# Edge pairs spread by TensorE, x loaded in parts, w0's products pipelined, and another order for the last tiles of a graph transformer's front

## The chip, the cores and the metric

The kernel runs on 1 core of a Trainium2 chip. The metric is device time in microseconds (us); smaller is better. Three runs of the kernel before took 3420.39, 3433.01 and 3434.41 us, median 3433.01.

## The reference

The inputs are x (2500 nodes x 512), and 40000 edges (src, dst), sorted by dst. What is computed:

```
deg  = max(number of edges into each node, 1);  norm = deg ** -0.5
h    = relu(layernorm(x))
x    = x + relu(norm * segment_sum((norm * (h @ w0))[src], dst) + bias0)
h    = relu(layernorm(x))
two layers, 8 heads of 64:
   q, k, v = h @ Wq.T + bq, h @ Wk.T, h @ Wv.T
   p = softmax over the edges of each target node of q[tgt].k[src] / 8
   h = batchnorm(h + segment_sum(p * v[src]) @ Wo.T + bo);  h = batchnorm(h + feed_forward(h))
out  = x + layernorm(h)
```

## The kernel before, in words

Nothing is gathered by edge. A matrix of counts (2500 x 2500, how often an edge src to dst occurs) is built in HBM, and it serves both parts: the first convolution is counts times hw, and the attention is dense, over all 2500 nodes, with log(count) added to the scores and a very low value where the count is zero.

The program has a front (function `front`, lines 191 to 907) and a transformer, which are blocks with a barrier between them. Nodes are handled in NT = 20 tiles of P = 125. The front has these stages.

1. **The matrix of counts.** DVE writes a tile of zeros (L533) and ScalarE's queue sends it to the table in HBM 8 times (L695, 25.0 MB in all). GpSimd then adds the edges to the table by 320 indirect DMAs of 125 edges each (L500), 160 groups of 2 on 2 sides of the table; the next group of a side waits until that side's last has landed, and the first waits until all zeros have. Each DMA needs cells and counts that `tallies(k)` on DVE makes (L509 to L531): 40 blocks of 8 columns. A column compares its 125 pairs (dst*2500+src) with the 250 pairs of its group (L518), which lie in `pair_row`, the same row in all 125 partitions. That row comes by DMA: the pairs are stored to HBM (`pair_flat`) and each block's 1000 pairs are loaded back by a DMA that repeats them over the partitions, two blocks in flight.
2. **Degrees and due times.** One-hot rows of dst (L555) are multiplied on TensorE (L809) for the degrees; `below` and `needed` (L565 to L588) work out which group is the last that a tile of nodes needs. As edges are sorted, tile t needs about 8(t+1) groups, 16(t+1) of the 320 indirect DMAs. The degrees go through HBM into column form (L704, L706), and norm follows (L598).
3. **h @ w0.** x is loaded whole by ScalarE's queue (L697), after the 8 issues of zeros and without a wait. Statistics of x (L577, L580), then a loop over tiles: ScalarE makes h (L716), TensorE turns it (L825), ScalarE copies it (L721), TensorE multiplies by w0 (L831), ScalarE scales the product into `hw` (L723), and only then begins the next tile. DVE meanwhile works off the tallies of blocks AHEAD = 5 to 39.
4. **The tile loop.** When all hw are there (`first_done`), SP loads w_q, w_k, w_v and three tiles of x, and then, for each tile t, the two halves of its count rows (`parts`, L114, "keys<-counts" in the trace), once GpSimd has landed the group that the tile needs. Two tiles are in flight. DVE merges the halves (L656), makes the bias of the attention (L665, L671), TensorE turns the counts (L843, 5 chunks) and multiplies them with hw (L853, 5 times 4 products of two passes), DVE finishes the convolution (L611 to L626), ScalarE normalises (L746). The projections of tile t-1 (L860, L871 twice, L879) stand between the chunks of tile t on TensorE. Results go to HBM: q, k, v in two f16 halves, the bias rows, x1.
5. **The end.** SP waits until tiles 0 to 17 are stored, fetches keys of heads 0 to 3 (L400) after the last merge, then keys of heads 4 to 7, and all values after the last product; tiles 18 and 19 go straight from SBUF to keys and values. `keys` and `values` lend their room to the front until then (w0, parts and cnt in keys, hw in values). At the end of the block SP waits for all bias, q and x1 stores and for the straight copies.

The attention begins with SP's load of q (L1208) and of 10 pieces of the bias (L1214). TensorE's first score waits for all keys, its first weighing for all values.

The order of each engine is written out by hand, and a later instruction of a queue is never run ahead of an earlier one that waits. On SP:

```
for t in range(NT + 3):
    store_bias(t - 2) ... store_q(t - 3), store_k(t - 3) ... store_x1(t - 2), store_v(t - 3)
    load_x(t + 1)
    sp.wait_ge(groups_landed, last_group)      # of tile t
    load_rows(sp, parts[t % 2] ...)
```

Of the kernel before, what the change touches and what calls it, by code (L numbers as in the profile page):

```python
# [17 lines left out]
F32 = mybir.dt.float32  # L18
F16 = mybir.dt.float16
BF16 = mybir.dt.bfloat16  # L20
# [9 lines left out]
D = 512  # L30
# [22 lines left out]

EARLY = 2
AHEAD = 5
# [81 lines left out]
def gnn_kernel(nc, x, src_cols, dst_cols, src_runs, dst_runs, w0, bias0, wq, wk, wv, wo, w1, w2,  # L137
# [17 lines left out]
    pair_flat = dram("pair_flat", [1, E], F32)  # L155
# [7 lines left out]
    with top:  # L163
# [10 lines left out]
        keys_early, keys_late = sem("keys_early"), sem("keys_late")  # L174
        values_early, values_late = sem("values_early"), sem("values_late")
# [4 lines left out]
def front(nc, sem, psum, sb, g):  # L180
    x, w0, bias0, xt = g["x"], g["w0"], g["bias0"], g["xt"]
    src_cols, dst_cols, src_runs, dst_runs = g["src_cols"], g["dst_cols"], g["src_runs"], g["dst_runs"]
    counts, bias_rows, x1_rows = g["counts"], g["bias_rows"], g["x1_rows"]
    pair_flat, deg_flat = g["pair_flat"], g["deg_flat"]
# [3 lines left out]
    keys_early, keys_late, values_early, values_late = g["keys_early"], g["keys_late"], g["values_early"], g["values_late"]  # L188
    XR = 4

    STRAIGHT = 2
    STAGED = NT - STRAIGHT
# [4 lines left out]
    HALVES = 2  # L197
    TH = NT // HALVES
# [5 lines left out]
    with ExitStack() as ctx:  # L204

        hw = values[:, :, :, :].rearrange("p h t e -> p (h t e)").bitcast(F32).rearrange("p (t d) -> p t d", t=NT)
        parts = [keys[0:P, 2 * b:2 * b + 2, :].rearrange("p h n -> p (h n)").bitcast(U16) for b in range(2)]
        cnt = [keys[0:P, 4 + 2 * b:6 + 2 * b, :].rearrange("p h n -> p (h n)").bitcast(F32) for b in range(2)]
# [14 lines left out]
        with ExitStack() as first:  # L223
            x_sb = sb(first, "x_sb", [P, NT, D])

            room = keys[:, :, :].rearrange("p h n -> p (h n)")
            w0_sb = room[:, 0:2 * FC * D].bitcast(F32).rearrange("p (c d) -> p c d", c=FC)
            room = room[0:EP, 2 * FC * D:].bitcast(BF16)
            onehot_hi = [room[:, b * QC * HI:(b + 1) * QC * HI].rearrange("p (c w) -> p c w", w=HI) for b in range(2)]
            room = room[:, 2 * QC * HI:]  # L230
            onehot_lo = [room[:, b * QC * LO:(b + 1) * QC * LO].rearrange("p (c w) -> p c w", w=LO) for b in range(2)]
            below = room[:, 2 * QC * LO:2 * QC * LO + TH * NCOL].rearrange("p (t c) -> p t c", t=TH)
# [5 lines left out]
            ramp_i = sb(first, "ramp_i", [EP, LO], I32)  # L238
            ramp = sb(first, "ramp", [EP, LO], BF16)
# [6 lines left out]
            src_run_i = sb(first, "src_run_i", [EP, NCOL], I32)  # L246
            dst_run_i = sb(first, "dst_run_i", [EP, NCOL], I32)
# [27 lines left out]
        with ExitStack() as first:  # L275
            deg_ps = psum(first, "deg_ps", [HI, LO])
            needed_ps = psum(first, "needed_ps", [NT, 2 * 128])
# [1533 lines left out]
```

## Time and profile before

| what | us |
|---|---|
| median of 3 runs | 3433.01 |
| the profiled execution | 3420.37 |
| its span in the profile | 3418.6 |
| TensorE busy | 3044.7 (89%) |
| GpSimd busy | 2156.7 (63%) |
| first indirect DMA begins | 72.96 |
| first h of the w0 loop | 130.64 |
| first merge of counts | 291.29 |
| last indirect DMA begins | 908.0 |
| attention's first product | 992.63 |

The page gives one execution. Busy time of an engine is summed over the whole span, so a stage must be read in windows. In a line of the timeline the numbers are the start, the length, the engine (a q behind it means its queue, which issues), the line, what is written and read, the count, and in brackets the idle time before it with what ended it.

### The profile page before, as it was taken

To read this page: it belongs to the slowest core of one execution; us is meant where nothing else is said; L and a number is where in the kernel's file an instruction comes from. 1 tells how busy PE (TensorE), PEld (TensorE's weight loads), DVE (VectorE), ACT (ScalarE), POOL (GpSimd) and SP (SyncE) were. 2 spreads that over 40 slices of the span, in tenths; PEclk is the share of its full clock that TensorE was granted. 3 is DMA by queue.
4 is the path that set the end of the run, shared out by engine and by line. 5 is a ranking of instruction groups with operands and counts; after the bars stand their busy time and mean duration, and the time that the engine had idled before them with its cause. 6 is when DMAs were issued, how large, how long until landed. Compare 5 with 4: busy or idle time off the path is not lost. (4 is left out here: it accounts for less than half of the span.)

```text
span 3418.6 us, 72329 instructions
## 1 busy us (share of the span) xinstructions
PE 3044.7 (89%) x24802; PEld 2394.4 (70%) x24802; DVE 2269.7 (66%) x6951; ACT 1953.9 (57%) x3918; POOL 2156.7 (63%) x1979
## 2 busy tenths in 40 slices
PE   2367999998769999999999989989999999999985
PEld 2123656654448888888888877767888888888874
DVE  8694344432237888888888853237888888888856
ACT  0123444443337778777777721227778778777734
POOL 1687888887527777777777710017777777777734
PEclk9998999998889999999999999999999999999998
DMA  9656666654479999999999821239999999889951
GB/s 372 99 129 139 122 133 117 125 104 90 111 181 175 165 170 169 166 166 175 165 163 165 152 74 31 54 72 175 168 165 168 168 171 170 166 163 168 158 122 60
DMA packets 1297433, 496.25 MB, mean 145 GB/s; under 512 B 1237211, under 2 KB 1262836, under 8 KB 1291379
## 3 DMA queue, kind: packets, MB, share of 16 engines
q1 hardware_dynamic: 1156168, 459.71, 67.3%
q0 software_dynamic: 133120, 0.80, 4.0%
q10 hardware_dynamic: 7788, 31.21, 2.8%
q8 instruction: 196, 3.21, 0.4%
q14 instruction: 161, 1.32, 0.1%
HBM read 153.04 MB, written 79.96 MB: 68 GB/s over the span
## 5 line engine op out<-in xcount | busy, mean ns | idle before, releaser
L1422 DVE CUSTOM_DVE_ANT_0 prob<-s_ps,mask 125x500 f32<-125x500 f32 x1600 | 1057.9, 673 | 286.0 <-PE s_ps L1267 207.9
L1199 POOL TENSOR_TENSOR staged<-prob,staged 125x500 f16<-125x500 f32 x960 | 1065.8, 1116 | 156.8 <-ACT staged L1193 94.7
L1359 ACT ACTIVATE prob<-prob,neg_max 125x1000 f32<-125x1000 f32 (+1 forms) x960 | 954.6, 994 | 114.5 <-DVE scrap L1428 112.8
L1267 PE MATMUL s_ps<-keys,queries 128*125 128x500 f16 x3200 | 945.7, 378 | 41.4 <-DMA queries<-q_tiles 29.2
L500 POOL DMA_INDIRECT counts<-count,cell x320 | 657.5, 2055 | 245.7 <-issue 107.5
L1300 PEld LDWEIGHTS o_ps<-values,across 125*125 125x125 f16 x7680 | 591.3, 138 | 200.5 <-issue 58.2
L1300 PE MATMUL o_ps<-values,across 125*125 125x128 f16 x7680 | 607.0, 222 | 38.2 <-DMA across<-staged 37.6
L1193 POOL CAST staged<-prob 125x500 f16<-125x500 f32 x640 | 385.6, 602 | 376.0 <-ACT prob L1359 252.8
L1435 DVE TENSOR_TENSOR p_lo<-t_ps,p_hi 125x500 f16<-125x500 f32 x640 | 432.0, 675 | 91.1 <-ACT p_hi L1369 90.8
L1278 PE MATMUL t_ps<-identity,prob 125*125 125x125 f32 x2560 | 412.5, 284 | 2.5 <-ACT agg L1379 2.2
L1369 ACT CAST p_hi<-t_ps 125x500 f16<-125x500 f32 x640 | 361.2, 564 | 85.9 <-PE t_ps L1278 85.6
L1267 PEld LDWEIGHTS s_ps<-keys,queries 128*125 128x125 f16 x3200 | 354.8, 139 | 54.5 <-DMA queries<-q_tiles 30.8
L853 PE MATMUL agg_ps<-values,turned 125*125 125x512 f32 x800 | 369.4, 605 | 4.3 <-ACT turned L730 3.4
L1300 PE MATMUL o_ps<-values,p_hi 125*125 125x128 f16 x2560 | 364.5, 221 | 1.5 <-DVE p_lo L1435 1.5
L1300 PE MATMUL o_ps<-values,p_lo 125*125 125x128 f16 x2560 | 363.4, 221 | 0.0
L1300 PEld LDWEIGHTS o_ps<-values,p_hi 125*125 125x125 f16 x2560 | 321.9, 137 | 51.6 <-DVE p_lo L1435 2.5
L1300 PEld LDWEIGHTS o_ps<-values,p_lo 125*125 125x125 f16 x2560 | 310.9, 138 | 47.0 <-issue 0.2
L1193 ACT CAST staged<-prob 125x500 f16<-125x500 f32 x320 | 195.7, 611 | 246.8 <-issue 188.5
L1278 PEld LDWEIGHTS t_ps<-identity,prob 125*125 125x125 f32 x2560 | 331.5, 189 | 6.0 <-ACT prob L1359 3.3
L853 PEld LDWEIGHTS agg_ps<-values,turned 125*125 125x125 f32 x800 | 145.6, 192 | 158.1 <-issue 157.6
L1248 POOL MEMSET staged<- 128x1024 f16 x6 | 5.5, 951 | 386.4 <-POOLq L999 308.6
L1359 ACT ACTIVATION_READ_ACCUMULATOR prob<-prob,neg_max 125x1 f32 x960 | 185.5, 193 | 0.0
(152 smaller groups left out, 3499.3 us busy)
## 6 DMA issues: line engine op xcount, KB each, us to landing
mask<-bias_rows SPq DMA_DIRECT2D x200, 218.8 KB
counts<-xt ACTq DMA_DIRECT2D x8, 3054.0 KB, 37.2
keys<-counts SPq DMA_DIRECT2D x40, 546.9 KB
bias_rows<-edge_bias SPq DMA_DIRECT2D x20, 1093.8 KB
queries<-q_tiles SPq DMA_DIRECT2D x80, 250.0 KB, 3.8
pair_row<-pair_flat SPq DMA_DIRECT2D x40, 437.5 KB
across<-staged SPq DMA_TRANSPOSE x960, 3.3
q_tiles<-q_both SPq DMA_DIRECT2D x80, 125.0 KB, 2.7
```

Source lines behind the costliest of these rows:

```text
L500: pool.indirect_dma_start(counts, bass.IndirectOffsetOnAxis(cell[:, c:c + 1], 0), count[:, c:c + 1], None, compute_op=ALU.add).then_inc(gr ...
L853: mm = pe.matmul(agg_ps[t % 2][0:P, :], lhsT=turned_sb[u % 2][0:P, j * P:(j + 1) * P], rhs=hw[:, s, :], start=(s == 0), stop=(s == NT - 1))
L1193: copy(staged[n % STAGES][0:P, 0:BPC, 0:P], prob[u % PROBS][:, k * KC:(k + 1) * KC].rearrange("p (s c) -> p s c", s=BPC)).then_inc(high_st ...
L1199: engine.tensor_tensor(here[0:P, BPC:2 * BPC, 0:P], prob[u % PROBS][:, k * KC:(k + 1) * KC].rearrange("p (s c) -> p s c", s=BPC), here[0:P ...
L1248: pool.memset(staged[r][:, :, :], 0).then_inc(stages_cleared, 1)
L1267: mm = pe.matmul(s_ps[n % SB][:, 0:KC], lhsT=queries[b][:, h, part, :], rhs=keys[:, h, c * KC:(c + 1) * KC], start=(part == 0), stop=(part ...
L1278: mm = pe.transpose(t_ps[r][0:P, s * P:(s + 1) * P], prob[u % PROBS][:, (k * BPC + s) * P:(k * BPC + s + 1) * P], identity[0:P, 0:P])
L1300: mm = pe.matmul(o_ps[u % 2][:, 0:2 * DH], lhsT=weights[:, s * step:s * step + P], rhs=values[:, u % H, k * BPC + s, :], start=(k == 0 and ...
L1359: act.activation(here, here, ACT.Exp, bias=neg_max[u % 4][:, :], accum_out=sums[u // H % 2][:, u % H, piece:piece + 1]).then_inc(exped, 1)
L1369: act.copy(p_hi[m % PB][:, :], t_ps[r][0:P, 0:KC]).then_inc(p_high, 1)
L1422: dve.tensor_tensor_reduce(out=prob[u % PROBS][:, at], in0=s_ps[n % SB][:, 0:KC], in1=bias[b][:, at], scale=1.0, scalar=MASKED, op0=ALU.ad ...
L1435: dve.tensor_tensor(p_lo[m % PB][:, :], t_ps[r][0:P, 0:KC], p_hi[m % PB][:, :], ALU.subtract).then_inc(bank_read, 1)
```

## The change

All of it is in `front`, but for two waits in the attention.

- Pairs' rows: the two extra loads of the edges, the store to `pair_flat` and 80 loads of `pair_row` (40 blocks in two cuts) are gone. TensorE makes a row of 500 pairs by 4 transposes of a column repeated 125 times, into two banks of PSUM, from which DVE's comparisons read. 80 such rows stand in TensorE's order, 30 ahead of the w0 loop and 50 inside it.
- x comes in four parts, issued after all zeros have landed, two in flight. DVE does the statistics of a part, then the tallies of a block. AHEAD goes from 5 to 10; 14 blocks are tallied ahead of h. The degrees' trip through HBM is issued by SP, early.
- The due times come from a smallest dst for each column, by transposes; the one-hot rows have their columns innermost.
- The w0 loop is skewed: ScalarE and TensorE turn tile t+1 before they multiply tile t. hw lies in the upper halves of keys and values, parts and cnt in the lower ones.
- SP loads the parts of tile 0 ahead of the weights and x, the parts of tile 1 behind them.
- From tile APART = 17 on, the projections of tile t-1 stand wholly ahead of the sums of tile t, on all engines.
- Only tile 19 goes straight to keys and values. Heads 0 and 1 are fetched when tiles 0 to 18 are stored, heads 2 and 3 after the last merge and the last bias, heads 4 to 7 after the last product. The first score waits for heads 0 to 3, the fifth unit's for the others.

The core of the diff:

```diff
-AHEAD = 5
+AHEAD = 10
+XPARTS = 4
+LAST_AHEAD = AHEAD + XPARTS - 1
-    STRAIGHT = 2
-    STAGED = NT - STRAIGHT
+    STAGED = NT - 1
+    APART = 17
 SP:
-                sp.wait_ge(pairs_ready, 1)
-                store_rows(sp, pair_flat.rearrange("o (p c) -> (o p) c", p=EP), pair_run[:, :], pairs_stored)
-                for k in range(NB):
-                    if k >= 2:
-                        sp.wait_ge(rows_used, k - 1)
-                    load_rows(sp, pair_row[k % 2][:, :], pair_flat[:, at].broadcast_to([EP, PER_ROW * GE]), rows_loaded[k % 2])
+                load_parts(0)
                 load_weights(sp, weights, 0, weights_loaded)
                 for t in range(XR - 1):
                     load_x(t)
+                load_parts(1)
+                for t in range(2, APART):
+                    store_bias(t - 2)
+                    if t >= 3:
+                        store_q(t - 3)
+                        store_k(t - 3)
+                    store_x1(t - 2)
+                    if t >= 3:
+                        store_v(t - 3)
+                    load_x(t + 1)
+                    load_parts(t)
+                store_q(APART - 3)
+                store_k(APART - 3)
+                store_v(APART - 3)
+                for t in range(APART, NT):
+                    if t == APART:
+                        store_bias(t - 2)
+                        store_x1(t - 2)
+                    if t + 1 < NT:
+                        load_x(t + 1)
+                    store_q(t - 2)
+                    store_k(t - 2)
+                    store_v(t - 2)
+                    store_bias(t - 1)
+                    store_x1(t - 1)
+                    load_parts(t)
+                store_q(NT - 2)
+                store_k(NT - 2)
+                store_v(NT - 2)
+                for b in range(2):
+                    sp.wait_ge(qkv_stored[b], QKV * len(range(b, STAGED, 2)))
+                keys_back(range(2), first_heads)
+                values_back(0, 2, first_heads)
+                sp.wait_ge(merged, NKC * NT)
+                keys_back(range(2, 4), first_heads)
+                store_bias(NT - 1)
+                values_back(2, 4, first_heads)
+                sp.wait_ge(cnt_t_used, NKC * NT)
+                keys_back(range(4, H), last_heads)
+                values_back(4, H, last_heads)
+                store_x1(NT - 1)
+                store_q(NT - 1)
+                keys_straight(NT - 1)
+                values_straight(NT - 1)
 DVE:
+                def tally_column(at):
+                    if at % RC == 0:
+                        dve.wait_ge(rows_turned, row + 1)
+                    dve.scalar_tensor_tensor(
+                        matches[at % 2][:, :], row_ps[row % 2][0:EP, own * GE:(own + 1) * GE], pair[:, at:at + 1],
+                        earlier[:, after:after + GE], ALU.is_equal, ALU.mult, accum_out=tally[:, at:at + 1]).then_inc(tallied, 1)
+                for part in range(XPARTS):
+                    x_statistics(part)
+                    if part + 1 < XPARTS:
+                        tallies(AHEAD + part)
+                for t in range(APART - 1, NT):
+                    if t >= APART:
+                        merge(t)
                         least(t)
                         mask(t)
                         convolve(t)
+                    low_q(t)
+                    low_k(t)
+                    low_v(t)
 ScalarE:
+                act.wait_ge(zeroed, 16 * ZDMAS)
+                for part in range(XPARTS):
+                    if part >= 2:
+                        act.wait_ge(x_loaded[part % 2], BOTH * (part // 2))
+                    load_rows(act, x_sb[:, tiles, :], x.rearrange("(t p) d -> p t d", p=P)[:, tiles, :], x_loaded[part % 2])
+                first_norm(0)
+                first_norm(1)
+                keep_ht(0)
+                for t in range(NT):
+                    if t + 1 < NT:
+                        keep_ht(t + 1)
+                    if t + 2 < NT:
+                        first_norm(t + 2)
+                    keep_hw(t)
 TensorE:
+                def spread_row(n):
+                    if n >= 2:
+                        pe.wait_ge(tallied, RC * (n - 1))
+                    for c in range(RC):
+                        mm = pe.transpose(row_ps[n % 2][0:EP, c * EP:(c + 1) * EP],
+                                          pair[:, n * RC + c:n * RC + c + 1].broadcast_to([EP, EP]), identity[0:EP, 0:EP])
+                    mm.then_inc(rows_turned, 1)
+                for t in range(NT):
+                    if t + 1 < NT:
+                        turn_h(t + 1)
+                    times_w0(t)
+                    for n in range(done + (NROW - done) * t // NT, done + (NROW - done) * (t + 1) // NT):
+                        spread_row(n)
+                def project_all(t):
+                    turn_x1(t)
+                    pe.wait_ge(xt_ready, t + 1)
+                    project(t, "wq_sb", q_ps, q_summed, q_scaled, FC)
+                    project(t, "wk_sb", k_ps, k_summed, k_low, 1)
+                    project_v(t)
+                for t in range(NT):
+                    between = 1 <= t < APART
+                    if t >= APART:
+                        project_all(t - 1)
 ...
+                project_all(NT - 1)
 attention, TensorE:
-                        pe.wait_ge(g["keys_early"], H * 16)
+                        pe.wait_ge(g["first_heads"], 4 * 16 + 2 * BOTH)
+                    if layer == 0 and u == H // 2 and c == 0:
+                        pe.wait_ge(g["last_heads"], 4 * 16 + BOTH)
-                    if layer == 0 and u == 0 and k == 0:
-                        pe.wait_ge(g["values_early"], 2 * BOTH)
```

## Rows read from the trace of the kernel before

**Rows 1.** SP's issues in the timeline, loads of parts of tiles 15 to 19

```profile
743.49 1.58 SPq L114 DMA_DIRECT2D keys<-counts  x4
...
869.43 1.58 SPq L114 DMA_DIRECT2D keys<-counts  x4
...
911.79 1.59 SPq L114 DMA_DIRECT2D keys<-counts  x4
```

**Rows 2.** L500 alone, 742 to 911 us: durations, starts, idle time before

```profile
L500 POOL DMA_INDIRECT counts<-count,cell x64: 1982/1986/2477, 742.1 to 908.0; - x64
...
  DMA counts<-count,cell: 15.0, 4
```

**Rows 3.** L500 alone, 318.6 to 742 us

```profile
L500 POOL DMA_INDIRECT counts<-count,cell x167: 1982/2000/2488, 318.6 to 739.8; - x167
```

**Rows 4.** Timeline of TensorE in the tile loop: turning of x1, tiles 1 and 11

```profile
353.36 0.59 PE L860 MATMUL x_ps<-identity,h 125*128 125x125 f32 x4
...
662.51 0.59 PE L860 MATMUL x_ps<-identity,h 125*128 125x125 f32 x4
```

**Rows 5.** Timeline of the start of the program and of the tile loop

```profile
72.96 2.13 POOL L500 DMA_INDIRECT counts<-count,cell  x1 [66.22 <-DMA counts<-xt]
...
107.91 11.96 DVE L577 BATCH_NORM_STATS2 stats<-x_sb 125x6 f32<-125x512 f32 x20 [22.23 <-DMA x_sb<-x]
...
130.64 0.81 ACT L716 ACTIVATE h<-x_sb,shift,rstd 125x512 f32<-125x512 f32 x1 [0.41 <-DVE norm L598]
...
291.29 3.04 DVE L656 TENSOR_TENSOR keys<-keys 125x500 f32<-125x500 uint16 x5 [21.85 <-DMA keys<-counts]
```

**Rows 6.** Windows: length, PE and PEld, DVE, ACT, POOL busy, clock, DMA share, GB/s

```profile
4.00:73.00 69.00, 18.95 (x321) 17.43 (x321) 66.26 (x108) 0.00 (x0) 2.78 (x5) 1.00 1.01 410
73.00:108.00 35.00, 0.00 (x0) 0.00 (x0) 6.96 (x37) 0.00 (x0) 12.52 (x7) 1.00 1.09 192
...
946.00:988.00 42.00, 20.64 (x92) 13.75 (x91) 6.12 (x12) 7.26 (x14) 0.22 (x1) 0.77 0.96 237
```

**Rows 7.** L500 alone, 80 to 110 us, and 0 to 277.5 us

```profile
  DMA counts<-count,cell: 21.3, 2
...
L500 POOL DMA_INDIRECT counts<-count,cell x77: 1982/2058/2212, 73.0 to 274.1; - x77
```

**Rows 8.** Timeline of GpSimd around first_done

```profile
284.28 1.99 POOL L500 DMA_INDIRECT counts<-count,cell  x1 [8.24 <-DMA counts<-count,cell]
...
297.51 2.00 POOL L500 DMA_INDIRECT counts<-count,cell  x1 [6.67 <-issue]
```

**Rows 9.** Timeline of TensorE, tile 18's sums

```profile
877.98 2.04 PE L843 MATMUL turn_ps<-identity,keys 125*125 125x125 f32 x8 [10.12 <-DVE keys L656]
879.94 5.45 PE L853 MATMUL agg_ps<-values,turned 125*125 125x512 f32 x8
...
907.85 3.60 PE L879 MATMUL v_ps<-wv_sb,xt 128*125 128x512 f32 x8
```

**Rows 10.** The same of tile 19's last steps, and the attention's first product

```profile
956.39 1.09 PE L860 MATMUL x_ps<-identity,h 125*128 125x125 f32 x4 [3.52 <-ACT h L746]
958.15 5.67 PE L871 MATMUL q_ps<-xt,wq_sb 128*128 128x125 f32 x32 [0.67 <-ACT xt L753]
...
967.24 3.60 PE L879 MATMUL v_ps<-wv_sb,xt 128*125 128x512 f32 x8
992.63 2.76 PE L1267 MATMUL s_ps<-keys,queries 128*125 128x500 f16 x6 [21.80 <-DMA queries<-q_tiles]
```

**Rows 11.** Timeline of DVE: tile 19's convolution, the last half of v

```profile
949.47 0.75 DVE L611 SCALAR_TENSOR_TENSOR conv<-agg_ps,norm,bias_sb 125x512 f32<-125x512 f32 x1 [2.15 <-PE agg_ps L853]
...
951.89 0.18 DVE L622 BATCH_NORM_AGGREGATE x_mv<-x_stats 125x2 f32<-125x6 f32 x1
...
971.49 0.69 DVE L643 TENSOR_TENSOR v_both<-v_ps,v_both 125x512 f16<-125x512 f32 x1 [2.77 <-ACT v_both L775]
```

**Rows 12.** Timeline of ScalarE: tile 19's root, before its h

```profile
954.80 0.29 ACT L744 ACTIVATE x_root<-x_mv,eps_col 125x1 f32<-125x1 f32 x1
```

More of the change, by code:

```diff
@@ L245, in front @@
             group_i = sb(first, "group_i", [EP, NCOL], I32)
-            src_run_i = sb(first, "src_run_i", [EP, NCOL], I32)
-            dst_run_i = sb(first, "dst_run_i", [EP, NCOL], I32)
-            pair_run = sb(first, "pair_run", [EP, NCOL])
-            pair_row = [sb(first, f"pair_row{b}", [EP, PER_ROW * GE]) for b in range(2)]
             matches = [sb(first, f"matches{r}", [EP, GE], BF16) for r in range(2)]
@@ L527, in tallies, with place_block @@
                                                         ALU.is_lt, ALU.mult))
-                    steps.wait(but=1)
-                    steps.done(dve.tensor_tensor(cell[:, at], moved[:, :], home[:, at], ALU.add))
+                def place_block(k):
+                    at = slice(k * BC, (k + 1) * BC)
                     steps.wait()
-                    dve.sem_inc(cells_ready, 1)
+                    dve.tensor_tensor(cell[:, at], moved[:, :], home[:, at], ALU.add).then_inc(cells_ready, 1)
@@ new lines, in tallies, with x_statistics @@
+                def tallies(k):
+                    for c in range(BC):
+                        tally_column(k * BC + c)
+                        if c == 2 and k >= 1:
+                            count_block(k - 1)
+                        if c == 4 and k >= 1:
+                            place_block(k - 1)
+                def x_statistics(part):
+                    dve.wait_ge(x_loaded[part % 2], BOTH * (part // 2 + 1))
+                    for t in range(part * XT, (part + 1) * XT):
+                        steps.done(dve.bn_stats(stats[:, t, :], x_sb[:, t, :]))
@@ L791, in _ @@
+                high_v(APART - 2)
+                for t in range(APART - 1, NT):
+                    if t >= APART:
+                        for k in range(3):
+                            chunk(t, k)
                         logarithm(t)
[L792 to L794 removed]
                         chunk(t, 3)
[L796 to L798 removed]
@@ L806, in _ @@
+                pe.wait_ge(consts_ready, 3)
+                pe.wait_ge(pairs_ready, 2)
+                spread_row(0)
+                spread_row(1)
+                for c in range(3):
+                    columns = slice(128 * c, min(128 * (c + 1), NCOL))
+                    mm = pe.transpose(dst_ps[0:columns.stop - columns.start, c * EP:(c + 1) * EP], dst[:, columns], identity[0:EP, 0:EP])
+                mm.then_inc(needed_turned, 1)
                 for q in range(QP):
```

381 lines of the change are left out of this document (187 added, 194 removed).

## The prediction

> **What bounds the kernel now.** I began with the loads of count rows on SP. The spacing of tiles 15 to 19 is (911.79 - 743.49) / 4 = 42.1 us [rows 1]. Further forward the spacing of two turnings of x1, ten tiles apart, is (662.51 - 353.36) / 10 = 30.9 us [rows 4], so there TensorE had work without a gap, and later it did not: tile 18's sums start after 10.1 us of idleness [rows 9]. Next I looked at GpSimd alone. An indirect DMA takes 1.99 us and 0.30 us to the next, 2.29 us as the floor; 167 of them take 423.5 us in the first stretch (2.54 each) and 64 take 167.9 us in the second (2.62 each), the last begins at 908.0 [rows 2, 3], and tile 19 is loaded 3.8 us later [rows 1]. A tile needs 16 of them, 16 x 2.62 = 42 us. So from about tile 12 on the scatter of edges sets the pace, and the end of the front is the end of the scatter and a tail: from tile 19's load at 911.8 to the attention's first product at 992.6, 80.8 us [rows 1, 10]. The scatter has one start, at 72.96, when the last zeros have landed [rows 5]. The reader should see in these rows that the chain of the front is zeros, 320 indirect DMAs, tail, and that x, tallies and the w0 loop lie beside it.
>
> How much slack lies there? TensorE could run the 19 tiles behind the first in 19 x 30.9 = 587 us, so from 291.3 [rows 5] the last would start at 878, and its counts come at 920 (911.8 and 8.1 to land and merge, by tile 18: 869.43 to 877.98 is 8.5) [rows 1, 9]. Some 40 us of the stage before the tile loop are covered already.
>
> **The change part by part.** The sum is made against the profiled execution, 3420.4 us with a span of 3418.6; the median of the three runs is 12.6 above it, and I add that at the end. About 0.5%, 17 us, is what a measurement of this kernel can tell from no change.
>
> *w0 loop, due times, one-hot rows, x in parts, seen from TensorE.* Now the loop runs from 130.6 to about 272. A tile's 8 products take 3.6 us at the full clock and up to 5.45 at the lower one [rows 9], say 4.2; 50 rows of 4 transposes stand in the new loop, at the 0.15 us of one of x1's four [rows 4] 30 us in all; with turning 0.6 us, 4.2 + 0.6 + 1.5 = 6.3 us a tile, 126 us, against 20 x 7.1. DVE's comparisons go on there, 26 blocks instead of 35, which now fit into the loop's 141 us, so at most 105 us, beside it; that they read PSUM now may lengthen them by a fifth before they bound the loop. The start moves from 130.6 to about 105: the statistics end at 119.9 [rows 5], of which x's landing gives some 10 us and their overlap with it another 9; what lies between them and h, 10.7 us, shrinks by the degrees' trip, which is made earlier. That puts first_done near 230, and with the parts of tile 0 ahead of 3 MB of weights the first merge near 240 instead of 291. All of these 50 us I cost at nothing: the cover is the scatter; if it were gone, the loop would end the front in both kernels and the 50 us would come through. Tile t of the loop starts at 240 + 30.9 t, its counts come at about 920 - 42 (19 - t); the two cross at tile 11, so eight or nine tiles go at the scatter's pace instead of four or five.
>
> *Zeros.* Until 73 the DMA engines are full (share 1.01, 410 GB/s) [rows 6]. 25.0 MB of zeros take 61 us of that; about 5 blocks of pair_row (2.4 MB) and the edges' loads go with them. Without pair_row, 2.4 / 0.41 = 6 us less: the scatter starts at 66.5. -6.5.
>
> *x beside the scatter's start.* From 73 to 108 the engines moved 6.7 MB [rows 6], x and w0 and about a megabyte of pair_row, and two indirect DMAs waited 21.3 us together [rows 7]. x is no longer queued before the scatter, but it is issued at the very time at which the scatter starts, so the same bytes less one in seven lie beside it. Bounds: nothing waits (-20.7), or no DMA lands for all 35 us (+8, as four would have gone in the 21.3 case beyond the waits). I take 21 x 6/7 = 17, -3.7, as nearest to the row.
>
> *Tallies beside the scatter.* From 73.0 to 274.1 there are 76 intervals, 174 us at the floor; of the 27 us more the two waits are 20.7, so 6.4 go to the time in which DVE tallies [rows 7]. Tallies end a fifth of that time earlier. -1.4.
>
> *The burst at first_done* (weights, x, parts) costs the scatter 8.24 + 6.67 less two gaps, 14.3 us [rows 8]. It stays. 0.
>
> *Tiles beside the scatter.* Over the floor, the first stretch lost 423.5 - 382.4 = 41 us to 13.7 tiles, 3.0 each, the second 167.9 - 146.6 = 21 us to 4 tiles, 5.3 each [rows 2, 3]: there the parts' load and all the stores of a tile come in one burst right behind a landing. With 8 instead of 4 tiles in that regime, +9.1.
>
> So tile 19's load moves by -6.5 - 3.7 - 1.4 + 9.1 = -2.5 us, to 909.3.
>
> *The last tiles' order.* Tile 16 is still interleaved. From its sums' start to the last add is 29.9 us and to the end of project_v 33.4 (877.98 to 907.85, where project_v starts, to 911.4) [rows 9]. From 17 on each tile is a serial ring: sums 20.1 us (first product at 1.5, 5 of 3.46, three turnings of 0.43; 22.4 where it begins cold as in [rows 9]), I take 21.2; then convolution, norm and h on DVE and ScalarE, 4.2 us (2.6 from 949.47 to the variance's end at 952.07, 1.6 from the root at 954.80 to the turning) [rows 11, 12]; then turning and three projections, 956.39 to 970.84, 14.4 us [rows 10]; then v's halves and the merge that DVE now makes behind them, 2.1 us (970.84 to 972.18, and 0.7) [rows 10, 11]. Sum 41.9 us, against the scatter's 42. Tile 17's sums start 8.5 + 29.9 + 4.2 + 14.4 + 2.1 + 2.8 (project_v of 15 before normalise) = 61.9 us after load 16, that is 19.9 after load 17, 11.4 later than its counts. As ring and pace are equal this lag stays: tile 19's sums end 19.9 + 21.2 = 41.1 us behind its load, where they now end at 949.4, 37.6 behind. +3.5. What was bought is that no other work lies in tile 19's sums, and it is paid for by the lag of tiles 17 and 18.
> The rows show the cost of such pauses: after 10.1 us of idleness the first 8 products take 5.45 us and later ones 3.60 [rows 9]; after 3.5 us of idleness q takes 5.67 [rows 10]. The Trainium skill (TensorE: Matmul & The Clock Gate, Why this matters for your kernels) says to leave no idle gaps between bursts of products, since the clock then falls from 2.4 to 1.2 GHz. The ring has two pauses a tile, 4.2 and 2.1 us; by the rule the cold values would hold for both, 22.4 + 4.2 + 14.4 + 2.1 = 43.1 us a ring, and the sums would end 3 us later still. This case's trace agrees for the pause of 3.5 us, and the mean granted clock there is 0.77 [rows 6].
>
> *After the last product.* Now 9.9 MB move between 946 and 988 (237 GB/s, share 0.96) [rows 6]: bias, half of the keys, all values, two tiles' q, k, v. The first product waits 21.8 us after the last projection [rows 10]. So DMA bounds this. In the new order keys and values of heads 0 and 1 and keys of 2 and 3 go earlier; behind the last product remain bias 1.25 MB, values of 2 and 3 1.2, heads 4 to 7 4.8, and 1.0 of q, k, v, x1: 8.25 MB, 32.6 us instead of 38.8 at the same rate. The block's end waits for the straight copies, which SP issues behind them on its queue, so that the later wait on heads 4 to 7 gives nothing of its own. 43.2 us from sums to first product become 37. -6.1.
>
> Sum: -2.5 + 3.5 - 6.1 = -5.1 us. The attention behind it is the same. 3420.4 - 5 = 3415, and on the median 3433 - 5 = 3428.
>
> **The rivals.**
> *A. The scatter goes at its better rate, and the lag is gone.* If tiles go on costing it 3.0 us and not 5.3 (8 x 2.3 = 18 us), or if the pace is slow enough to swallow the lag (sums at 8.5 + 21.2 = 29.7 us behind the load, -11.4), or if x in parts frees the scatter (-17), the sum is -17 to -23 with one, some -35 with two. For it: the 5.3 rests on 4 tiles, and the new order splits the stores of the last three. Against: [rows 7, 8] show waits wherever the queues are full. At two of them: 3398.
> *B. The scatter is held up more.* Place: GpSimd's wait on the landing of its last group. x starts with it, and the tile loop starts 50 us earlier beside it. If the full 35 us are lost (+9 on my 17) and every tile costs 5.3 (10 x 2.3 = 23), the sum is -5 + 32 = +27, 3460; half of it gives +11, 3444. It decides from 2.59 us per DMA behind first_done: my tile costs, 72 us over about 255 DMAs, make 2.57, and 5 us more turn the sign.
> *C. The earlier tile loop comes through.* If the scatter did not bound, its 50 us would be added: 3428 - 50 = 3378. Against: 10.1 us of idleness before each late tile [rows 9] and 42 us spacing. At 2.29 us each with all its waits gone the scatter would end some 60 us earlier; only then.
>
> **How the numbers follow.** The forecast (within 17 us of before) 0.58; A far enough to be over 0.5%, 0.27; C 0.03; B over 0.5%, 0.12. So faster 0.30, same 0.58, slower 0.12. The range takes A with two of its terms and half of B: 3398 to 3444.
>
> **What would show it.** First indirect DMA at 66 to 67; its idle time behind landings between 66 and 105 near 17 us; last one at 903 to 910; first merge near 240 and TensorE idle before tiles 11 to 16; tile 17's sums 20 us behind its load; the last product 41 us behind tile 19's load; the attention's first product 37 us after it. I am wrong on the pace if the mean of a late indirect DMA is not 2.6 us, wrong on the ring if tile 19's sums start within 12 us of its load, and wrong on the bound if SP never waits for GpSimd in tiles 12 to 19.

## The result and the profile after

The kernel after takes 3438.63 us (median of 19 runs, 3429.04 to 3446.74), the kernel before on the same chip 3421.27 (19 runs). The ratio is 1.0048, 95% interval 1.0038 to 1.0059: slower by half a per cent, where 3428 (5 us less, too little to tell from no change) had been forecast. The profiled execution took 3441.34 us, span 3439.5, granted clock 0.968 (before 0.969).

First the front, stage by stage. GpSimd's indirect DMAs in the timeline of the kernel after, against [rows 5, 7]:

```profile
67.12 2.13 POOL L529 DMA_INDIRECT counts<-count,cell  x1 [55.33 <-DMA counts<-xt]
...
84.25 1.97 POOL L529 DMA_INDIRECT counts<-count,cell  x1 [8.15 <-DMA counts<-count,cell]
...
93.87 1.96 POOL L529 DMA_INDIRECT counts<-count,cell  x1 [5.37 <-DMA counts<-count,cell]
```

L529 alone, 527 to 911 us, against [rows 2, 3]:

```profile
L529 POOL DMA_INDIRECT counts<-count,cell x144: 1963/1982/2427, 527.1 to 900.7; - x144
...
  DMA counts<-count,cell: 41.5, 14
```

The scatter starts at 67.1 instead of 73.0, is held up by x in pieces of 8.2 and 5.4 us, and its late DMAs come every (900.7 - 527.1) / 143 = 2.61 us. Its last one begins at 900.7, 7.3 us earlier than before. TensorE and SP at the end of the front, against [rows 1, 9, 10]; first SP's loads of tiles 17 to 19, then TensorE:

```profile
830.51 1.70 SPq L119 DMA_DIRECT2D keys<-counts  x4
...
866.72 1.58 SPq L119 DMA_DIRECT2D keys<-counts  x4
...
907.87 1.58 SPq L119 DMA_DIRECT2D keys<-counts  x4
```

```profile
840.12 1.29 PE L959 MATMUL turn_ps<-identity,values 125*125 125x125 f32 x8 [1.99 <-DVE values L702]
...
881.13 1.29 PE L959 MATMUL turn_ps<-identity,values 125*125 125x125 f32 x8 [1.99 <-DVE values L702]
...
922.12 1.29 PE L959 MATMUL turn_ps<-identity,values 125*125 125x125 f32 x8 [1.99 <-DVE values L702]
923.57 3.67 PE L969 MATMUL agg_ps<-keys,turned 125*125 125x512 f32 x8 [0.17 <-ACT turned L796]
...
941.26 1.02 PE L969 MATMUL agg_ps<-hw_last,turned 125*125 125x512 f32 x2
946.54 1.09 PE L976 MATMUL x_ps<-identity,h 125*128 125x125 f32 x4 [4.26 <-ACT h L812]
948.31 5.79 PE L987 MATMUL q_ps<-xt,wq_sb 128*128 128x125 f32 x32 [0.67 <-ACT xt L819]
...
957.50 3.60 PE L995 MATMUL v_ps<-wv_sb,xt 128*125 128x512 f32 x8
980.58 2.76 PE L1393 MATMUL s_ps<-keys,queries 128*125 128x500 f16 x6 [19.48 <-DMA queries<-q_tiles]
```

The attention begins at 980.6 instead of 992.6 [rows 10]. So the front got 12 us shorter, and still the whole got 21 us longer. Cut at the first products of attention and feed-forward of each layer:

| stage, us | before | after | |
|---|---|---|---|
| front, to the first score | 992.6 | 980.6 | -12.0 |
| attention of layer 0 | 1005.1 | 1022.4 | +17.3 |
| feed-forward of layer 0 | 292.2 | 291.3 | -0.9 |
| attention of layer 1 | 1002.6 | 1019.2 | +16.6 |

In the attention nothing was changed but where two waits stand, and the whole of it is slower in both layers. The windows of 800 us, from 100 us behind the first score, before and after (columns: length, PE, PEld, DVE, ACT, POOL busy, clock, DMA share, GB/s):

```profile
1092.60:1892.60 800.00, 786.06 (x8214) 676.17 (x8213) 665.08 (x2139) 628.45 (x1350) 590.91 (x657) 1.00 0.93 167
```

```profile
1080.70:1880.70 800.00, 774.96 (x8064) 666.02 (x8063) 653.04 (x2097) 615.82 (x1322) 581.38 (x645) 1.00 0.94 164
```

Every engine does 1.8 to 2.1% fewer instructions in the same time, at a granted clock of 1.00, and each is idle more. What TensorE waits for is in the page's costliest groups (busy, mean ns | idle before, and its releaser), before and after:

```profile
L1300 PE MATMUL o_ps<-values,across 125*125 125x128 f16 x7680 | 607.0, 222 | 38.2 <-DMA across<-staged 37.6
...
L1278 PE MATMUL t_ps<-identity,prob 125*125 125x125 f32 x2560 | 412.5, 284 | 2.5 <-ACT agg L1379 2.2
```

```profile
L1424 PE MATMUL o_ps<-values,across 125*125 125x128 f16 x7680 | 609.1, 223 | 53.7 <-DMA across<-staged 52.5
...
L1404 PE MATMUL t_ps<-identity,prob 125*125 125x125 f32 x2560 | 413.1, 284 | 10.5 <-ACT agg L1503 10.3
```

The same products take the same time; the DMA transposes of the probabilities (`across<-staged`, 960 of them) come later. TensorE's two waits grew by 15.5 and 8.0 us, 23.5 of the 34 us that the two layers lost. The question for the experiments is how a change of the front slows transposes that begin after it has ended.

### The profile page after: what moved, and what is told of

Its sections match the earlier page's. It is cut to its first block and busy times, and to the rows that moved or that the text cites. A ratio compares the mean times of both kernels' runs of the same rounds, so it can differ in the third digit from the quotient of the medians.

```text
span 3439.5 us, 72920 instructions
## 1 busy us (share of the span) xinstructions
PE 3127.9 (91%) x25127; PEld 2476.6 (72%) x25127; DVE 2237.3 (65%) x6932; ACT 1955.9 (57%) x3918; POOL 2155.8 (63%) x1981
## 5 line engine op out<-in xcount | busy, mean ns | idle before, releaser
L529 POOL DMA_INDIRECT counts<-count,cell x320 | 647.1, 2022 | 243.8 <-issue 112.0
L969 PE MATMUL agg_ps<-values,turned 125*125 125x512 f32 x400 | 180.9, 592 | 0.0
L1446 PE MATMUL t_ps<-agg,wo_sb 128*128 128x125 f32 x1280 | 178.8, 284 | 1.1 <-ACT agg L1503 1.1
```

Source lines behind the costliest of these rows:

```text
L529: pool.indirect_dma_start(counts, bass.IndirectOffsetOnAxis(cell[:, c:c + 1], 0), count[:, c:c + 1], None, compute_op=ALU.add).then_inc(gr ...
L969: mm = pe.matmul(agg_ps[t % 2][0:P, :], lhsT=turned_sb[u % 2][0:P, j * P:(j + 1) * P], rhs=hw(s), start=(s == 0), stop=(s == NT - 1))
L1446: mm = pe.matmul(t_ps[r][:, 0:P], lhsT=wo_sb[:, k, o * 128:(o + 1) * 128], rhs=agg_t[t % 2][:, k * P:(k + 1) * P], start=(k == 0), stop=(k ...
```

## The experiments

**What moved by accident.** The change also freed three semaphores and two inputs, and took a table out of HBM, so that everything else may lie elsewhere there. Each was put back alone, the third with its two loads, and the table of the kernel before was moved. The code is cut to the lines that count.

```diff
 e1, on the kernel after
+        spare = [sem(f"spare{i}") for i in range(3)]
 e2, on the kernel after
+    pair_flat = dram("pair_flat", [1, E], F32)
 e3, on the kernel after
+                load_rows(sp, run_i[:, 0, :], g["dst_runs"], runs_loaded)
+                load_rows(sp, run_i[:, 1, :], g["src_runs"], runs_loaded)
 e4, on the kernel before
-    pair_flat = dram("pair_flat", [1, E], F32)
     (behind q_tiles instead)
+    pair_flat = dram("pair_flat", [1, E], F32)
```

> The changed kernel with three unused semaphores allocated ahead of the attention's, so that every semaphore of the attention has the number that it had before. The front of the changed kernel is 12 us shorter, and each attention layer (first score to first product of the feed-forward) is 16 to 17 us longer though its code is the same. Theory numbers (the semaphores' numbers matter): both attentions come back to 1005 us, total about 33 us under the changed kernel, 0.988 to 0.994 of before. Theory placement in HBM, and theory phase (the attention starts otherwise): no change against the changed kernel, 1.003 to 1.007 of before, attention layer 0 at 1022.

> The changed kernel with the HBM tensor pair_flat (160 KB) still declared but unused, so that x1, keys, values and q lie at the same offsets in HBM as before. Theory placement of internal tensors: attention layers back to 1005 us each, 0.988 to 0.994 of before. Theories numbers and phase: nothing moves, 1.003 to 1.007.

> The changed kernel, which also loads the two input tensors that only the kernel before read (four small DMAs at the start, nothing uses them), so that the program has the same inputs again and HBM is laid out with them. Theory placement of inputs: attention layers back towards 1005 us, 0.988 to 0.995 of before. Theories numbers and phase: 1.003 to 1.007, as the four loads cost under 1 us at the start.

> The kernel before with pair_flat declared behind q_tiles, so that x1, keys, values and q lie 160 KB lower in HBM, as in the changed kernel. Theory placement of internal tensors: attention layers of 1016 to 1024 us in place of 1005, 1.006 to 1.010 of before. Any other theory: 0.998 to 1.002.

Measured: ratios to before of 1.0067 (1.0048 to 1.0086), 1.0041 (1.0021 to 1.0062), 1.0067 (1.0041 to 1.0093) and 1.0011 (0.9995 to 1.0027). The attention's layers take 1023.3 and 1021.8, 1018.9 and 1018.9, 1021.3 and 1022.4 us in the first three, 1003.5 and 1001.9 in the fourth. Neither semaphores, nor addresses in HBM, nor the inputs make the loss; all three theories fell. The expectations name a fourth, phase: that the attention begins at another time. The table below speaks against it: at remainder 88 the first score comes anywhere from 976.1 to 1003.8 us, and the layers stay between 996 and 1007.

**Looking closer at the slow transposes.** The list of DMA queues on the page has rows that I had passed over. Before and after:

```profile
q8 instruction: 196, 3.21, 0.4%
q14 instruction: 161, 1.32, 0.1%
```

```profile
q8 instruction: 199, 3.26, 0.4%
q14 instruction: 161, 1.32, 0.1%
```

The engines' instructions themselves come over the DMA engines. A packet of q8 is 3.21 MB / 196 = 16 KB and takes 1.03 us in the median, where a packet of a transpose (256 B) takes 18 ns. The page counts 24802 products and as many weight loads of TensorE before and 25127 after, so there is one such packet for about 256 TensorE instructions: in the attention one each 12.1 us in the median. I then took the trace's records of the transposes' packets from the first score on, over 2290 us, by the time since the nearest packet of q8, and counted those that took over 0.7 us:

```
us from a fetch of q8   before: packets, slow    after: packets, slow    f2 (below): packets, slow
0 to 1                  45199    1435  3.2%      44151    1600  3.6%     38958    1221  3.1%
1 to 2                  43610     372  0.9%      39532     591  1.5%     43753     453  1.0%
all others, -6 to +6   843495     390  0.05%    824324     393  0.05%   850713     446  0.05%
```

Eight slow packets in ten stand in the 2 us behind a fetch of instructions, which hold one packet in ten. One unit of the attention (a head of a tile) has 128.7 TensorE instructions, two have 257.4: nearly the 256 of a fetch. So the fetch moves by only 1.4 instructions from one cycle of two units to the next, about 112 in the 80 cycles of a layer, and where it starts depends on how many instructions TensorE has run before the attention. That is 6744 before, 88 modulo 256, and 650 more after, 7394, 226 modulo 256: the transposes of the pairs' rows are TensorE's, and each is a product and a weight load (640 of the 650). The traces bear the place out. The 41st fetch of layer 0 lies 119 TensorE instructions behind the first score of its two units in the kernel before and 20 behind it in the kernel after.

**Adding instructions that do nothing.** Waits on a semaphore that has long been there, nothing else:

```diff
+def idle(engine, g, count):
+    for i in range(2 * count):
+        engine.wait_ge(g["consts_ready"], 3)
 f1: SP, ahead of its wait for deg_ready      idle(sp, g, 83)
 f2: TensorE, over tiles 11 to 15             idle(pe, g, ...), 374 in all
 f3: the kernel before, TensorE, 45 to 120 us idle(pe, g, 300) and idle(pe, g, 350)
 f4: f1 and f2, and DVE 110, ScalarE 124, GpSimd 126
```

(`count` becomes that many instructions.) f2 brings the kernel after to the remainder 88 of before, f3 brings the kernel before to the 226 of after. The 41st fetch of layer 0 then lies at 123 in f2 and at 18 in f3.

 The attention's instructions are the same in both kernels; what lies ahead of them on each engine is not (SP 83 fewer, TensorE 650 more, DVE 18, ScalarE 4, GpSimd 2 more). Here the changed kernel gets 83 already satisfied waits on SP, so that SP's instructions of the attention lie where they lay before. Theory instruction position, of SP: attention layers back from 1020 to about 1004 us, total 0.994 to 0.998 of before. If SP's position doesn't matter: 1.003 to 1.007, layers 1018 to 1023.

> The changed kernel with 374 instructions on TensorE that only wait on something long met, 75 in each of tiles 11 to 15, in its idle time there (51 ns each, 3.8 us of some 10 idle): 650 + 374 = 1024, so the attention's instructions of TensorE lie as before in relation to blocks of 256 (and of 1024). Theory instruction position, of TensorE: attention layers back to about 1004 us, total 0.994 to 0.998 of before. If not TensorE's: 1.003 to 1.007, layers 1018 to 1023.

> The kernel before with 650 such waits on TensorE in its idle time from 45 to 120 us, so that the attention's instructions of TensorE lie where they lie in the changed kernel. Theory position of TensorE: attention layers of 1018 to 1023 us in place of 1004, total 1.007 to 1.011 of before. If not TensorE's: 0.998 to 1.002, layers 1002 to 1006.

 Theory instruction position, of any engine or of several together: attention layers back to about 1004 us, total 0.993 to 0.998 of before, which beats both kernels. If the attention stays at 1018 to 1023 here too, the position within a block is not the cause, and something that the front leaves behind (its order of DMAs) is.

The page's first line shows that 374 instructions were added to the 72920 of after:

```profile
span 3396.9 us, 73294 instructions
```

and f2's rows for the two groups above, and its window:

```profile
L1431 PE MATMUL o_ps<-values,across 125*125 125x128 f16 x7680 | 606.3, 222 | 30.7 <-DMA across<-staged 30.1
...
L1411 PE MATMUL t_ps<-identity,prob 125*125 125x125 f32 x2560 | 412.1, 283 | 3.5 <-ACT agg L1510 3.5
```

```profile
1079.80:1879.80 800.00, 788.74 (x8239) 678.35 (x8238) 668.43 (x2145) 630.27 (x1353) 590.80 (x660) 1.00 0.94 168
```

The kernel with 374 instructions more is about 1% faster than the one without (ratios to before of 0.9942 and 1.0048): 8239 products in 800 us instead of 8064, 30 instead of 53 us of waiting for transposes. The waits themselves cost the front nothing (first score at 979.8, 980.6 without them), but it was closer than expected: a record lasts 51 ns, yet two of them start 106 ns apart, so 75 fill 7.9 us of TensorE's 8 to 10 idle us and not 3.8. The kernel before becomes slow by the opposite edit; its window:

```profile
1089.00:1889.00 800.00, 778.70 (x8107) 669.04 (x8106) 655.20 (x2108) 619.97 (x1330) 585.24 (x649) 1.00 0.93 165
```

**The curve, and two parts of the change.** Two further remainders, 24 (310 waits) and 152 (438); then two parts of the change undone on top of f2, at an equal number of TensorE instructions.

```diff
 g1, g2: as f2, with 310 and 438 waits
 g3, on f2 (a guard around load_x is left out)
-    APART = 17
+    APART = NT
+                store_bias(NT - 2)
+                store_x1(NT - 2)
                 store_q(APART - 3)
 g4, on f2
-                keys_back(range(2), first_heads)
-                values_back(0, 2, first_heads)
                 sp.wait_ge(merged, NKC * NT)
-                keys_back(range(2, 4), first_heads)
+                keys_back(range(4), first_heads)
                 store_bias(NT - 1)
-                values_back(2, 4, first_heads)
                 sp.wait_ge(cnt_t_used, NKC * NT)
                 keys_back(range(4, H), last_heads)
+                values_back(0, 2, first_heads)
+                values_back(2, 4, first_heads)
                 values_back(4, H, last_heads)
-                    if layer == 0 and u == H // 2 and c == 0:
+                    if layer == 0 and u == 0 and c == 0:
                         pe.wait_ge(g["last_heads"], 4 * 16 + BOTH)
```

> The kernel after with 310 TensorE waits in tiles 11 to 15 instead of 374: 7704 instructions of TensorE ahead of the attention, 24 modulo 256 (374 waits gave 88, as the kernel before has; the kernel after has 226). If the place of the fetch in the cycle of two attention units decides (257.4 instructions, a fetch every 256), the cost is a smooth function of the remainder: 24 lies 54 from 226 and 64 from 88, so each layer's attention should take something between 1000 and 1020 us, I expect about 1010, and the median about 3418. Rival: any added waits in tiles 11 to 15 help, whatever their number: then 3397 and 1000 us per layer, as with 374. A third: it is only the exact address 88 that is good: 1018 or more and 3431.

> The kernel after with 438 TensorE waits there: 7832 ahead of the attention, 152 modulo 256, 64 beyond the good place and 74 short of the bad one. By the place of the fetch each layer should take between 1000 and 1020 us, about 1010, and the median about 3418; with the run at 24 this gives four points of the curve (24, 88, 152, 226). By the rival (any added waits help) 3397 and 1000 us per layer. If the slow packets of the transposes stand under TensorE's fetches here too, near 90% of them lie within 3 us of one, and their number within the first 1000 us of attention goes with the layer's time (1120 at 1000 us, 1386 at 1020).

> 374 waits as in the fastest version, but the last tiles' order undone: the projections of tiles 16, 17 and 18 stand between the chunks of the next tile, as in the kernel before, in the same number of instructions. In the kernel after tile 19's sums end 34.3 us behind its load, and the attention's first product comes 38.4 us after the last projection. With the old order the sums should end about 37.6 us behind the load as in the kernel before (+3.3), and heads 0 and 1, which then can only be fetched after tile 18's projections inside tile 19's sums, move into the time after the last product: 3.4 MB of 8.2 more there at 240 KB per us, at most +10. I expect the attention 8 us later than with 374 waits alone (987 instead of 979.8), each layer 1000 us, and the median 3405. Rival: the order bought nothing, 3397 and the attention at 980. If the attention's layers go to 1010 or more though TensorE's count is the same, the place of the fetch isn't all that decides.

> 374 waits as in the fastest version and the new order of the last tiles, but the early fetches undone: keys of heads 0 to 3 after the last merge, everything else (keys of 4 to 7 and all values) after the last product, and the first score waits for all of it, as in the kernel before. That puts 9.9 instead of 8.2 MB behind the last product by my count, so by my theory the attention starts 4.8 us later (the 43.2 and 38.4 us measured between last product and first score), 984.6 instead of 979.8, and the median is 3402. Rival: bias rows and straight copies bound the end whatever is fetched when, 3397 and 980. Each layer stays at 1000 us by both, as TensorE's count is the same.

All of them together, sorted by the remainder (first score, attention of layers 0 and 1 in us, each from one profiled execution; the ratio is to the kernel before on the same chip, while medians of different groups of runs come from different chips):

| run | remainder | first score | layer 0 | layer 1 | median | ratio (95%) |
|---|---|---|---|---|---|---|
| g1 | 24 | 982.9 | 1011.0 | 1009.3 | 3422.2 | 0.9993 (0.9983 to 1.0003) |
| f2 | 88 | 979.8 | 1000.0 | 998.3 | 3396.8 | 0.9942 (0.9917 to 0.9967) |
| f4 | 88 | 978.9 | 1000.0 | 995.6 | 3396.9 | 0.9943 (0.9919 to 0.9967) |
| g3, old order | 88 | 1003.8 | 998.4 | 1001.4 | 3426.1 | 1.0009 (0.9996 to 1.0022) |
| g4, late fetch | 88 | 976.1 | 1006.5 | 1001.6 | 3413.5 | 0.9964 (0.9953 to 0.9975) |
| before | 88 | 992.6 | 1005.1 | 1002.6 | 3421.3 | |
| e4 | 88 | 995.7 | 1003.5 | 1001.9 | 3422.8 | 1.0011 (0.9995 to 1.0027) |
| g2 | 152 | 976.8 | 1014.5 | 1008.7 | 3420.1 | 0.9986 (0.9970 to 1.0002) |
| after | 226 | 980.6 | 1022.4 | 1019.2 | 3438.6 | 1.0048 (1.0038 to 1.0059) |
| e1 | 226 | 976.7 | 1023.3 | 1021.8 | 3441.6 | 1.0067 (1.0048 to 1.0086) |
| e2 | 226 | 975.3 | 1018.9 | 1018.9 | 3433.8 | 1.0041 (1.0021 to 1.0062) |
| e3 | 226 | 976.4 | 1021.3 | 1022.4 | 3441.6 | 1.0067 (1.0041 to 1.0093) |
| f1 | 226 | 977.1 | 1019.3 | 1012.6 | 3430.0 | 1.0050 (1.0034 to 1.0066) |
| f3 (before) | 226 | 988.5 | 1019.2 | 1015.8 | 3447.8 | 1.0096 (1.0065 to 1.0128) |

What follows:

- Every run at 88 has layers of 996 to 1007 us, every one at 226 of 1013 to 1023, whichever front it has, and 24 and 152 lie between, 1009 to 1015 (only f1's layer 1 overlaps with them). The places of the 41st fetch go with it: 105 to 123 in the six runs at 88, 4 to 20 in the six at 226, 241 in g1 and 46 in g2. That any added wait helps is out (g1, g2 and f3), that only other engines' instructions matter too (f1 changes little, f4 adds nothing to f2). The number of instructions that TensorE runs ahead of the attention makes the loss. That it counts modulo 256 rests on the fetches in the trace; 6744 and 7768, the only numbers tried at 88, also agree modulo 512 and 1024, and no run separates these.
- It may not be all: among runs of one remainder up to 10 us a layer remain. Each figure is one execution, and 19 executions of the kernel after alone spread over 17.7 us, so this can be the spread between executions. g4's layer 0 is 6.5 us longer than f2's at the same count, against what both theories of that run said, and f1's layer 1 is 3 to 10 shorter than that of the others at 226. f1 adds SP instructions, so that fetches of other engines (q14) may have a part; that stays open. So does how a fetch holds a transpose up: what was moved is the instruction count, and that the packets are late just behind a fetch is what the records show; a fetch itself could not be taken away.
- g1 and g2 came close to what was expected of them (layers of 1010, medians of 3418). In g2 90% of the slow packets lie within 3 us of a fetch, as expected, but their number follows the time only loosely. In the first 1000 us of attention there are 1147 in f2, 1193 in g2, 1242 in g1 and 1386 in the kernel after, yet also 1238 in g3 and 1299 in g4, whose layers are short.
- g3: with the old order the sums of tile 19 end at 944.0, 37.0 us behind its load at 906.9, where f2 has 34.7: +2.3 of the +3.3 expected. But the first score comes 59.8 us behind them instead of 38.7, 24 us later in all and not 8: no head can be fetched until v of tile 18 is stored (950.7 here), and it is made behind tile 19's sums. With the new fetches the old order costs 24 us. What it costs with the old fetches no run shows.
- g4: late fetches cost 42.5 us from the last sum (933.6) to the first score instead of 38.7, +3.8 of the +4.8 expected. The last indirect DMA began 4.5 us earlier in this run than in f2, which is why its attention doesn't start later.

f2 is, with f4, the best version found: 0.9942 of before, and 0.9942 / 1.0050 = 0.989 of f1, which is the kernel after with 83 waits on SP, on the same chip (by the medians alone 0.995 and 0.990).

## Why the prediction was wrong

The step that failed is one sentence: "The attention behind it is the same." Its code, its operands and its instructions are the same, its place in TensorE's stream of instructions is not, and that cost 17.3 + 16.6 = 34 us, nearly three times what the whole change gains in the front. The sum had no term for it, and no rival had it; all three looked at the front alone. Of the 650 instructions 640 were in plain sight, "50 rows of 4 transposes" in the prediction and 30 rows before them in the description of the change, and they were priced only at the time that they take.

For the front the forecast was -5.1 and the trace shows -12.0: tile 19's load -3.9 (forecast -2.5), the sums behind it -3.2 (forecast +3.5), the end behind them -4.9 (forecast -6.1). Step by step:

- *Zeros*: first indirect DMA at 67.1, forecast 66.5. Right.
- *x beside the scatter*: three waits of 13.8 us together up to 105 us, forecast 17. Near enough; the 17 was itself a slip, as 21 x 6/7 is 18.
- *w0 stage*: the first h comes at 119.9, not near 105. DVE is the cause and not x: it tallies almost without a pause from 73 to 92.2, and a block of tallies of 3.3 us stands between each two of the four parts of the statistics. The loop then takes about 118 us, forecast 126; a row of four pair transposes takes 0.60 us, as the prediction had it, and 8 products take 3.60 us where it allowed 4.2. The first merge is at 250.9, forecast 240. Tiles go at the scatter's pace from tile 13 on, and not from 11 as forecast, but the cover held: TensorE is idle for 8.5 to 10.1 us before the sums of tiles 13 to 16 (3.4 before tile 12's), so these 11 us cost nothing, as the argument said.
- *Tiles beside the scatter*: 2.61 us per late DMA, forecast 2.6. The last begins at 900.7; 908.0 - 2.5 = 905.5 was forecast. Tile 19 is loaded at 907.9 (forecast 909.3): SP issues it 7.2 us behind the start of the last indirect DMA, where it was 3.8 before.
- *The ring of the last tiles*: tile 17's sums start at 840.1, which is 61.9 us behind load 16 at 778.2, to the tenth of what the prediction worked out. But they start 9.6 us behind their own load, where 20 had been forecast: SP issues load 17 at 830.5, 52.3 us behind load 16, and it doesn't wait for GpSimd there at all. It comes late through its own queue, which holds the stores of tile 15's v and of tile 16's bias and x1 first. SP's waits from 800 to 912 us, loads 17 to 19 (us in all, times, longest), for DVE's bias of the tile ahead (L717) and for GpSimd's landed groups:

```profile
SPq L124 <- DVE edge_bias L717: 37.3, 2, 18.9
...
SPq L119 <- POOLq L533: 1.5, 1, 1.5
SPq L119 <- POOLq L527: 1.2, 1, 1.2
```

So at loads 18 and 19 SP waits for the scatter only 1.2 and 1.5 us, where before it waited 24 us at each. The prediction let the ring follow the loads; it left out that the loads follow the ring too, through SP's stores of the tile ahead. The ring is (922.12 - 840.12) / 2 = 41.0 us, forecast 41.9. The lag then shrank, from the 19.9 of the forecast to 922.1 - 907.9 = 14.3 us behind tile 19's load: the three loads from 16 to 19 took 129.7 us and not 126, which swallows 3.7, and two rings 1.8 less. Sums of 20.2 instead of 21.2 give 1 more. So the sums end 34.4 us behind the load, not 41.1; the term was -3.2 and not +3.5. The serial ring was there with the forecast's length; the size of its lag hung on a difference of two numbers near 42.

- *The clock in the ring*: x1's turning behind the pause of 4.3 us runs at a granted clock of 0.50, the lower of the two levels (1.2 GHz), and q behind it takes 5.79 us at a mean of 0.64. Behind the pause of 2.0 us the first 8 products of the sums take 3.67, at 1.00 (2.4 GHz). The three windows are x1's turning, q and those products:

```profile
946.50:948.00 1.50, 1.09 (x4) 0.71 (x4) 0.00 (x0) 0.32 (x1) 0.00 (x0) 0.50 0.86 305
948.30:954.10 5.80, 5.79 (x34) 5.79 (x35) 0.00 (x0) 0.00 (x0) 0.00 (x0) 0.64 1.03 241
923.50:927.30 3.80, 3.73 (x11) 1.83 (x12) 2.66 (x7) 0.52 (x1) 0.00 (x0) 1.00 0.50 152
```

So the ring of 43.1 us that low values at both would have made did not come. The Trainium skill (TensorE: Matmul & The Clock Gate, Why this matters for your kernels) warns of idle gaps between bursts, but only of gaps above a size; the prediction left that off when it put the rule on both pauses. The trace agrees with the page for the longer pause.

- *After the last product*: 38.3 us from 942.3 to the first score, forecast 37, before 43.2. Right within 1.3 us, and g4 shows that 3.8 of the 4.9 saved come from the early fetches. The working was less good than its result: 9.9 and 8.25 MB at the 237 GB/s of its row take 41.8 and 34.8 us, and not the 38.8 and 32.6 that it sets against each other.

Rival A (better rate, lag gone) came true in part in the front: 7 us less in the ring, and the last indirect DMA 5 us earlier than forecast, of which only 1.4 reached tile 19's load. B and C did not happen: the scatter was held up as forecast, and it still comes last at loads 18 and 19, though by 1.2 and 1.5 us only. Had the attention kept its 2007.7 us for two layers, the median would have been 3438.6 - 33.9 = 3405 where before takes 3421, 0.5% faster; f2, with layers of 1000 and 998, shows 3397 where before took 3413. The 3428 of the forecast stood on a median of three runs, 3433.01; against the 3421.27 of 19 runs its -5 us would read 3416.

So the small difference of the medians says nothing about the parts: -12 in the front, +34 behind it, -1 in between.

## What to carry to other kernels

Cut both traces at the same points before explaining a difference of half a per cent: here the part that was changed gained 12 us and the part that was not lost 34. When code that wasn't touched slows down, look at what it shares with the rest, the stream of instructions too, and add a few hundred instructions that do nothing in front of it: if that moves the time, the change's own merit can only be judged with both kernels at the same remainder, or each at its best. When the instruction count of a loop, or of two rounds of it, nearly equals that of a fetch, the fetch creeps through the loop slowly and a long stretch can run at a bad place; padding ahead of it is a knob worth 1% here.

## What the runs showed of the hardware that was not expected

- Instructions of TensorE arrive as 16 KB packets over the DMA engines, one for about 256 instructions, each about 1.0 us long; in the 2 us behind one, 2.0 to 2.6% of the transposes' 256 B packets take over 0.7 us, elsewhere 0.05%.
- 374 waits that wait for nothing made a kernel about 1% faster, and 650 made another 1.0% slower.
- The 320 one-hot products of the degrees have the same shapes in both kernels, but what TensorE reads as a column lies apart in memory after the change, with another column's numbers between: 242 ns in the median before, 319 after; they start 53 and 133 ns apart. That the distance makes the difference wasn't tried by itself. The two lines alone, before and after:

```profile
L809 PE MATMUL deg_ps<-keys x320: 238/242/243, 14.0 to 47.3; 125*40 125x64 bf16 x160
```

```profile
L902 PE MATMUL deg_ps<-keys,values x320: 317/319/336, 15.2 to 57.8; 125*40 125x64 bf16 x160
```
